# The first pass of a four-layer graph kernel multiplies h, turned, by the adjacency matrix, and its weights follow

## What is computed

```python
A2 = A + eye; dscale = diagonal(A2) ** -0.5
temp = A2 @ h @ W0.T                                   # pass 0
x = x + relu((dscale[:,None] * A2 * dscale[None,:]) @ temp)      # pass 1
g = h @ weight; gn = g / norm(g)
x = x + softmax(gn @ gn.T + log(adj + eps)) @ g + bias          # attention pass (2)
rowsum = adj.sum(axis=1); di = rowsum ** -0.5
x = x + relu((di[:,None] * adj * di[None,:]) @ h @ W + b)        # pass 3
# passes 4 and 5: two layers of relu(concat([h, adj @ h]) @ W), added to x once
```

## Time and profile before

| | us |
|---|---|
| runs, median of 3 (lowest to highest) | 2330.94 (2330.2 to 2331.07) |
| the profiled execution, its own time | 2330.06 |
| its span, first to last instruction | 2328.3 |
| pass 0, first product to the first of pass 1 | 21.89 to 390.28 |
| pass 1, to its last matmul | 390.28 to 741.31 |
| mean granted TensorE clock | 0.998 |

### The profile page before, as it was taken

One profiled execution on the slowest core, in us unless ns is written; L12 is line 12 of the kernel. 1 busy time (PEld: TensorE's weight loads), 2 busy tenths in 40 slices (PEclk: granted clock), 3 DMA queues, 4 the chain that ended last, 5 costly groups with the idle time before them and its releaser, 6 DMA issues.

```text
span 2328.3 us, 62880 instructions
## 1 busy us (share of the span) xinstructions
PE 2301.6 (99%) x24536; PEld 1937.0 (83%) x24536; DVE 1718.5 (74%) x2765; ACT 1130.9 (49%) x1821; POOL 140.3 (6%) x114
## 2 busy tenths in 40 slices
PE   7999999999999999999999999999999999999999
PEld 7888888666665677678888899999988888899998
DVE  7887876777776877678888876776776767666665
ACT  6644433454554555555555555555544444433332
POOL 2211101111010000000000000000000000000000
PEclk9999999999999999999999999999999999999999
DMA  8799998888987889989999998898898898999997
GB/s 288 218 359 340 356 357 305 253 270 272 275 266 222 252 294 286 277 282 305 330 312 327 330 363 307 327 342 304 327 345 320 333 339 301 340 347 378 375 371 292
DMA packets 291738, 726.86 MB, mean 312 GB/s; under 512 B 76704, under 2 KB 109728, under 8 KB 258848
## 3 DMA queue, kind: packets, MB, share of 16 engines
q1 hardware_dynamic: 291328, 724.42, 89.8%
q10 hardware_dynamic: 288, 0.79, 0.1%
HBM read 574.64 MB, written 138.41 MB: 306 GB/s over the span
## 4 chain that ended last, share of the span: by engine, by line
PE 91%; DVE 4%; issue 3%; POOL 1%; ACT 0%; POOLq 0%; DVEq 0%; ACTq 0%
PE acc L949 9%; PE acc L977 8%; PE acc L974 8%; PE acc L978 8%; PE acc L952 8%; PE acc L954 8%; PE acc L953 8%; PE acc L950 5%; PE acc L964 4%; PE acc L967 4%; PE acc L966 4%; PE psS L1198 2%; PE psS L1200 2%; PE psS L1199 2%; DVE alo L2115 1%
## 5 line engine op out<-in xcount | busy, mean ns | idle before, releaser
L952 PE MATMUL acc<-right,ahi 128*128 128x258 f16 x1536 | 420.0, 273 | 5.7 <-DVE alo L2115 2.3
L954 PE MATMUL acc<-right,alo 128*128 128x258 f16 x1536 | 419.9, 273 | 0.0
L953 PE MATMUL acc<-right,ahi 128*128 128x256 f16 x1536 | 419.3, 273 | 0.0
L974 PE MATMUL acc<-left,ahi 128*128 128x128 f16 x1536 | 270.4, 219 | 0.4 <-DVE alo L1746 0.4
L978 PE MATMUL acc<-left,alo 128*128 128x128 f16 x1536 | 270.4, 219 | 0.0
L977 PE MATMUL acc<-left,ahi 128*128 128x128 f16 x1536 | 270.4, 219 | 0.0
L1608 ACT ACTIVATE ahi<-en 128x512 f16<-128x512 f32 x256 | 160.2, 626 | 75.2 <-DVE en L2100 73.1
L952 PEld LDWEIGHTS acc<-right,ahi 128*128 128x128 f16 x1536 | 150.4, 98 | 38.2 <-DVE alo L2115 7.8
L949 PE MATMUL acc<-left,ahi 128*128 128x512 f16 x512 | 180.2, 379 | 0.0
L949 PE MATMUL acc<-left,en 128*128 128x512 f16 x512 | 180.2, 379 | 0.0
L978 PE MATMUL acc<-left,adj 128*128 128x128 f16 x1024 | 178.1, 219 | 0.0
(11 more groups left out here) (273 smaller groups left out, 6542.9 us busy)
## 6 DMA issues: line engine op xcount, KB each, us to landing
adj<-in_adj_t SPq DMA_DIRECT2D x192, 512.0 KB, 5.9
adj<-ready SPq DMA_DIRECT2D x96, 1024.0 KB, 7.7
en<-ready SPq DMA_DIRECT2D x96, 1024.0 KB, 8.1
adj<-in_adj_t SPq DMA_DIRECT2D x32, 1024.0 KB, 8.6
en<-in_adj_t SPq DMA_DIRECT2D x32, 1024.0 KB, 9.1
en<-ready SPq DMA_DIRECT2D x64, 512.0 KB, 5.2
en<-sent SPq DMA_DIRECT2D x46, 512.0 KB, 7.1
sent<-en SPq DMA_DIRECT2D x90, 256.0 KB, 4.3
```

The costliest lines, as they stand in the source:

```text
L952: nc.tensor.matmul(acc[:, b, 0:n], hi, m[:, jb, 0:n], start=first, stop=False)
L953: nc.tensor.matmul(acc[:, b, 0:F], hi, m[:, jb, LO:LO + F], start=False, stop=False)
L954: return nc.tensor.matmul(acc[:, b, 0:n], lo, m[:, jb, 0:n], start=False, stop=last)
L974: nc.tensor.matmul(to, hi[:, rows], bhi[:, cols], start=first and i % 2 == 0 and b == 0 and k == 0, stop=False, skip_group_check=True)
```

## The change

- Pass 0 multiplies by h itself. The block of h (128 rows x 128 features) is the stationary operand and adj's transpose the moving one, 512 columns at a time, so the result comes out turned, z = (adj h) transposed, in two banks per row group, and the row groups take the four banks in turn (`turned_block`). eye is added on PE by `own_rows`: 16 matmuls of 128 columns per row group by 256 times the identity. No transposes, no copy.
- z is split (ACT `hi_of_z`, DVE `lo_of_z`) at chunk 0 of the next row group, multiplied by W0 behind chunk 2 (24 matmuls), and the result, scaled by d, split at chunk 3 (`hi_of_t`, `lo_of_t`).
- The first two row groups (PAIRED) are taken in turn: each 512 rows of h serve a chunk of both. The statistics run one round ahead, and the splits of a round stand in front of the rows of the next. ACT makes the normalised rows of rounds 1 to 7 too.
- Pass 1 has the three matmuls of 258, 256 and 258 columns; the row sums move there, and with them POOL's power and `inverse_rows`; ACT alone takes its result out of the banks. CROSS and `add_cross` go.
- Two blocks of similarity (AHEAD) are made before the last chunk of pass 1.
- SP issues the first chunk at once, in two halves, and weights and diagonal between later chunks. keep_warm is 40 matmuls.

```diff
-WARM = [60, 60]
+WARM = 40
+PAIRED = 2
 LEAD = 3
+AHEAD = 2
...
+def pairs():
+    load_at(0)
+    load_x(1)
+    load_at(1)
+    load_at(2)
+    load_x(2)
+    load_at(3)
+    load_x(3)
+    for n in range(4, PAIRED * NC):
+        load_at(n)
+        if n < 8:
+            load_x(n)
+            load_weight(n - 4)
+        elif n == 8:
+            load_weight(4)
+            load_biases()
+        if n % 2 == 1 and n >= 9:
+            load_diagonal((n - 9) // 2)
+        store_whole(*place_of(n - 4))
...
-        both = m[:, jb, :].rearrange("p (s n) -> p s n", s=2)[:, :, 0:F]
-        nc.tensor.matmul(acc[:, b, :].rearrange("p (s n) -> p s n", s=2), hi, both, start=first, stop=False)
-        return nc.tensor.matmul(acc[:, b, 0:F], lo, m[:, jb, 0:F], start=False, stop=last)
     n = F + 2
     nc.tensor.matmul(acc[:, b, 0:n], hi, m[:, jb, 0:n], start=first, stop=False)
...
+def turned_block(g, n, c, k, f):
+    hi, lo = moving_of(n, k)
+    rows = mov[0][:, GB * c + k, :]
+    bhi, blo = rows[:, f * P:(f + 1) * P], rows[:, LO + f * P:LO + (f + 1) * P]
+    to = acc[:, 2 * (g % 2) + f, :]
+    nc.tensor.matmul(to, bhi, hi, start=c == 0 and k == 0, stop=False, skip_group_check=True)
+    nc.tensor.matmul(to, bhi, lo, start=False, stop=False, skip_group_check=True)
+    return nc.tensor.matmul(to, blo, hi, start=False, stop=False, skip_group_check=True)
+def own_rows(g):
+    for f in range(FB):
+        for b in range(GB):
+            rows = mov[0][:, GB * g + b, :]
+            to = acc[:, 2 * (g % 2) + f, b * P:(b + 1) * P]
+            nc.tensor.matmul(to, rows[:, f * P:(f + 1) * P], scaled_ident[:, :], start=False, stop=False,
+                             skip_group_check=True)
+            nc.tensor.matmul(to, rows[:, LO + f * P:LO + (f + 1) * P], scaled_ident[:, :], start=False, stop=False,
+                             skip_group_check=True)
+def first_pass():
+    for n in range(NG * NC):
+        g, c = place_of(n)
+        if n == 0:
+            pe.wait_ge(first_split, 1)
+        else:
+            pe.wait_ge(split_ready, n + 1)
+        if g == 0:
+            pe.wait_ge(mov_ready, at(MOVE, PRE, c, GB, 1 if c < 3 else GB))
+        if c == NC - 1:
+            if n == chunk_no(0, 0, NC - 1):
+                pe.wait_ge(scaled_ident_ready, 1)
+            own_rows(g)
+        for k in range(GB):
+            if g == 0 and c < 3 and k > 0:
+                pe.wait_ge(mov_ready, at(MOVE, PRE, c, GB, k + 1))
+            if n == 0 and k == GB // 2:
+                pe.wait_ge(split_ready, 1)
+            for f in range(FB):
+                if c == 0 and k == 0 and g >= PAIRED:
+                    pe.wait_ge(ev_ready, at(ALL, 0, g - 2, GB, 2 * f + 2))
+                last = turned_block(g, n, c, k, f)
+                if c == NC - 1 and k == GB - 1:
+                    last.then_inc(acc_ready, 2)
+        if c < NC - 1:
+            last.then_inc(chunk_done, 1)
+        if g >= PAIRED and c == 2:
+            if n == PAIRED * NC + 2:
+                pe.wait_ge(w_ready, 1)
+            step("W0W1", 0, g - 1 if g > PAIRED else 0)
+        if g == PAIRED and c == 6:
+            step("W0W1", 0, 1)
...
-            if tp in SMALL and tp != PRE and (c, b) in PLACES:
+            if p == 1 and isinstance(g, int) and g == NG - 1 and (c, b) == (NC - 2, GB - 1):
+                for j in range(AHEAD):
+                    similarity(0, j)
...
-keep_warm(WARM[0])
-pe.wait_ge(w_ready, 1)
-pe.wait_ge(ones_ready, 1)
-for s in ["T0T1", "W0", "W1"]:
-    step(s, PRE, 0)
-keep_warm(WARM[1])
-step("T0T1", PRE, 1)
+keep_warm(WARM)
...
+def hi_of_z(g, side):
+    if not (isinstance(g, int) and g == 0):
+        act.wait_ge(small_ready, at(SMALL, 0, g - 1, 2, 2))
+    for f in range(FB):
+        act.wait_ge(acc_ready, at(ALL, 0, g, GB, 2 * f + 2))
+        nc.scalar.activation(hTq[:, f, :, :], acc[:, 2 * side + f, :].rearrange("p (b n) -> p b n", n=P),
+                             ACT.Copy, scale=1.0 / ADJ_SCALE).then_inc(h_hi, GB // FB)
+def hi_of_t(g):
+    act.wait_ge(d_w_ready, 1)
+    for r in range(2):
+        act.wait_ge(small_ready, at(SMALL, 0, g, 2, r + 1))
+        for b in (2 * r, 2 * r + 1):
+            nc.scalar.activation(mov[1][:, blocks(g, b), 0:F], small_out(0, b), ACT.Copy,
+                                 scale=d_w[:, blocks(g, b)]).then_inc(mov_hi, 1)
...
+def first_rows(g):
+    act.wait_ge(shift_ready, at(NORM, PRE, g))
+    if g >= 2:
+        act.wait_ge(mov_ready, at(MOVE, PRE, g - 2, GB, GB))
+    u = g % 2
     for b in range(GB):
-        nc.scalar.activation(mov[1][:, blocks(g, b), 0:F], o[:, b, :], ACT.Copy, scale=d[:, blocks(g, b)])\
+        args = dict(bias=shift[:, u, b:b + 1], scale=rstd[:, u, b:b + 1])
+        nc.scalar.activation(mov[0][:, blocks(g, b), 0:F], xres[:, GB * g + b, :], ACT.Relu, **args)\
             .then_inc(mov_hi, 1)
+        if g > 0:
+            nc.scalar.activation(normed_of(g)[:, b, :], xres[:, GB * g + b, :], ACT.Identity, **args)\
+                .then_inc(normed, 1)
...
+TWO_PLACES = {0: ("z", 0), 3: ("t", 0), 4: ("z", 1), 7: ("t", 1)}
+def first_group(g, side):
+    for c in range(NC):
+        split(0, g, c)
+        if isinstance(g, int) and g == PAIRED:
+            if c in TWO_PLACES:
+                first_tail(*TWO_PLACES[c], TWO_PLACES[c][1])
+        elif c in FIRST_PLACES:
+            first_tail(FIRST_PLACES[c], g - 1, 1 - side)
+        if isinstance(g, int) and g == PAIRED + 1 and c == 5:
+            hi_of_weights(slice(wofs[1], wofs[5]), w_loaded, 16 * 5)
...
-stage("h", PRE, 0)
-hi_of_weights(slice(0, wofs[1]), w0_loaded, 16)
+act.wait_ge(const_ready, 1)
+nc.scalar.activation(rowm[:, :], neghalf[:, 0:GB], ACT.Copy)
 split(0, 0, 0)
+first_rows(0)
 for q in range(NG):
-    keep_hT(q, 0)
-    keep_hT(q, 1)
-    stage("W0", PRE, q)
-    if q == 0:
-        stage("W1", PRE, q)
+    split(0, 1, q)
     if q + 1 < NG:
-        stage("h", PRE, q + 1)
-    if q > 0:
-        stage("W1", PRE, q)
-    if q != 1:
-        split(0, 0, max(1, q))
-hi_of_weights(slice(wofs[1], wofs[5]), w_loaded, 16 * 4)
+        split(0, 0, q + 1)
+        first_rows(q + 1)
+    if q == NG - 2:
+        hi_of_weights(slice(0, wofs[1]), w_loaded, 16 * 5)
+first_group(PAIRED, 0)
+first_group(PAIRED + 1, 1)
+with act.Fori(PAIRED + 2, NG, 2) as g:
+    first_group(g, 0)
+    first_group(g + 1, 1)
...
+def lo_of_z(g, side):
+    for f in range(FB):
+        dve.wait_ge(h_hi, at(SMALL, 0, g, GB, 2 * f + 2))
+        nc.vector.scalar_tensor_tensor(hTq[:, FB + f, :, :],
+                                       acc[:, 2 * side + f, :].rearrange("p (b n) -> p b n", n=P), 1.0 / ADJ_SCALE,
+                                       hTq[:, f, :, :], ALU.mult, ALU.subtract).then_inc(ev_ready, GB // FB)
+    dve.wait_ge(ev_ready, at(ALL, 0, g, GB, GB))
...
+def lo_of_first_rows(g):
+    if g < 3:
+        for b in range(GB):
+            dve.wait_ge(normed, at(NORM, PRE, g, GB, b + 1))
+            dve.wait_ge(mov_hi, at(MOVE, PRE, g, GB, b + 1))
+            row = mov[0][:, GB * g + b, :]
+            nc.vector.scalar_tensor_tensor(row[:, LO:LO + F], normed_of(g)[:, b, :], 0.0, row[:, 0:F],
...
-for name in ["stats", "norm", "h"]:
-    stage(name, PRE, 0)
-lo_of_weights(slice(0, wofs[1]), 1)
+dve.wait_ge(const_ready, 3)
+nc.vector.tensor_scalar(scaled_ident[:, :], ident[:, :], ADJ_SCALE, None, ALU.mult).then_inc(scaled_ident_ready, 1)
+stage("stats", PRE, 0)
+split_first(0, first_split, first_hi)
+stage("norm", PRE, 0)
+lo_of_first_rows(0)
+split_first(1, split_ready, split_hi)
 stage("stats", PRE, 1)
-split(0, 0, 0)
 for q in range(NG):
-    if q == 0:
-        stage("W0", PRE, q)
-        stage("W1", PRE, q)
-    if q + 1 < NG:
-        stage("norm", PRE, q + 1)
     if q > 0:
-        stage("W0", PRE, q)
-    if q + 1 < NG:
-        stage("h", PRE, q + 1)
-    if q > 0:
-        stage("W1", PRE, q)
-    if q + 2 < NG:
+        split(0, 0, q)
+    if q == 1:
+        lo_of_first_rows(1)
+        stage("stats", PRE, 2)
+    elif q == 2:
+        stage("stats", PRE, 3)
+        lo_of_first_rows(2)
+    elif q > 2 and q + 2 < NG:
         stage("stats", PRE, q + 2)
-    if q != 1:
-        split(0, 0, max(1, q))
-lo_of_weights(slice(wofs[1], wofs[5]), 2)
+    split(0, 1, q)
+    if q == 2:
+        stage("stats", PRE, 4)
+    if q > 1 and q + 1 < NG:
+        lo_of_first_rows(q + 1)
+    if q == NG - 2:
+        lo_of_weights(slice(0, wofs[1]), 1)
 dve.wait_ge(diag_loaded, 16 * GB)
 nc.vector.tensor_scalar(diag[:, :], diag[:, :], 1.0, None, ALU.add).then_inc(diag_one, 1)
+dve.wait_ge(d_ready, 1)
+nc.vector.tensor_scalar(d_w[:, :], d[:, :], 1.0 / W_SCALE, None, ALU.mult).then_inc(d_w_ready, 1)
+first_group(PAIRED, 0)
+first_group(PAIRED + 1, 1)
+with dve.Fori(PAIRED + 2, NG, 2) as g:
+    first_group(g, 0)
```

(43 more changed lines are left out.)

346 lines of the change are left out of this document (174 added, 172 removed).

## The result

The changed kernel takes **2322.23 us** (median of 6 runs, 2321.43 to 2322.64) against 2330.32 (6 runs of before beside them): ratio 0.9965, 95% interval 0.9955 to 0.9975, 8.1 us faster. The forecast was 2323, with a range from 2314 to 2335. The profiled execution took 2322.25 us with a span of 2320.4.

A forecast was written before the change was run, and what follows sets the result against it. PE, busy in 99% of the span, was the bound. Terms 12.0 + 357.3 + 8.7 + 1.0 + 0.7 + 357.6 ended pass 1 at 737.3 against 741.4; with 3.5 at the next step, 7.6 us faster: 2323, range 2314 to 2335.

The forecast's parts named there:

- first product of pass 0: Start of the kernel: PE's first useful product at 12.0 us, bounds 10.7 and 13.5, 9.9 us sooner than before.
- stalls of the paired rounds: First two row groups of pass 0: PE waits 8.7 us together, bounds 3 and 17.
- half clock behind them: Pass 0's paired rounds: waits of 2 us and more may lower PE's clock, taken as 1.0 us.
- later row groups: Six later groups of pass 0: splits at chunks 1 and 4 cost 0.7 us, bounds 0 and 6.
- saved at the step to attention, clock included: From pass 1 to attention: 2.1 us of shorter wait and 1.4 of avoided half clock, 3.5 together.
- power of the diagonal: Ahead of row group 2: DVE waits for POOL's power of the diagonal, 5.43 us, costing PE 0.9.
- From the third round on DMA may set the pace: Paired rounds: splits wait for queued stores; stalls to round 4 are 5.3 us in all at 390 GB/s.
- the diagonal's four loads: nothing: Paired rounds 4 to 7: each load stands 4.4 us ahead of a store; costs nothing, or 4 if landing takes 12.
- What is left after the last chunk: ... 2.1 saved: Step to attention: 2.5 us remain after pass 1's last chunk, against 4.65 without the moved blocks.
- supply at 352 GB/s: Rival, paired rounds: loads and stores never go faster, stalls reach 17 us, 2333, about no change; chance 0.18.
- rounds set by handoffs: Rival, paired rounds: ACT and DVE waiting on each other make a round 12.8 us instead of 10.4; 2341; chance 0.10.
- No gain at the step: Rival, step to attention: PE waits as long for the exponential ahead of the last chunk as after it; 2326.5; chance 0.04.

The follow-up runs named there:

- e4: Changed kernel with x's first 512 KB issued by SP ahead of the first chunk, instead of by ACT beside it; 2321.31 us.
- e6: Changed kernel with ACT making a round's rows ahead of the split of its first chunk, from round 3 on, DMAs untouched; 2318.27 us.
- e7: Changed kernel with three edits: rows ahead of the split, diagonal's loads at chunks 12 to 15 and biases at 12, x's first rows ahead on SP; 2315.76 us.
- e10: e7 with DVE's lo of the second chunk put ahead of round 1's statistics, its sums behind them; 2317.75 us.
- e3: Changed kernel with the diagonal's four loads at chunks 12 to 15 (before 9, 11, 13, 15) and biases at 12 (before 8); 2319.59 us.
- e1: Changed kernel with AHEAD = 0, no block of similarity before the last chunk of pass 1; 2322.72 us.
- e8: Kernel before, with pass 1 by three matmuls of 256 columns and DVE's addition gone, similarity blocks left behind pass 1; 2329.91 us.
- e5: Kernel before, with only AHEAD = 2 added: two similarity blocks before the last chunk of pass 1; 2327.93 us.
- e2: Changed kernel with the five weight loads (1.75 MB) issued with chunks 9 to 13 of the pairs instead of 4 to 8; 2321.99 us.
- e9: Changed kernel with two edits: rows ahead of the split from round 3 on, and x's first rows ahead of the first chunk on SP; 2317.57 us.

## Why the prediction was right, point by point

The sum of the profiled executions, forecast and measured:

| term | forecast | measured |
|---|---|---|
| first product of pass 0 | 12.0 | 12.97 |
| PE's work in pass 0 | 357.3 | 357.2 |
| stalls of the paired rounds | 8.7 | 6.66 |
| half clock behind them | 1.0 | 1.40 |
| later row groups | 0.7 | 0.68 |
| PE's work in pass 1 | 357.6 | 358.0 |
| end of pass 1, without the moved blocks | 737.3 | 736.9 |
| saved at the step to attention, clock included | 3.5 | 3.4 |

The measured work of pass 0 is 378.90 - 12.97 less the 8.74 of the three rows below it; that of pass 1 is 739.30 - 378.90 less 2.38 for the moved blocks. The step is 2.38 + 2.46 = 4.84 us for 6.95, 2.1 saved, and 1.3 of clock. Against the kernel before, the first product comes 8.9 us sooner, PE's work of pass 0 is 3.2 shorter (360.4 by the prediction's sum) and its waits 0.7 longer, pass 1 is 6.9 longer, and the step with its clock 3.4 shorter: 7.9 in all, the difference of the two spans.

Part of the match is luck: the start came 1.0 us later than forecast and the stalls of the paired rounds 2.0 shorter, and the half clock behind them, forecast with 1.0, was 1.40 in this execution and 0 in others with longer stalls (e4).

- **PE's work** held to 0.1 us in pass 0: 512 columns with h stationary take 0.216, and `own_rows` 0.89 us a group for the forecast 0.90. Over passes 0 and 1 together PE's work grew, as argued; the gain is at the start and at the step to attention.
- **The start** was 1.0 us later, and one term has it: sharing the engines with the first chunk was taken as 1.2 us and cost 2.2 (x's statistics at 6.56 for 4.39). POOL's power took 2.04 for the forecast 2.3. The 40 matmuls of no use took 4.05 us, from 8.92 to 12.97, and ended about 0.2 behind the first rows' lo (about 12.8, as DVE's lo of the rows starts at 12.23 and PE followed that start by 0.56 to 0.57 wherever it waited for it: e4, e6, e7, e10).
- **The stalls by hand**: second chunk 1.17 for 1.6, rows of round 2 0.87 for 0.9, later rounds 4.62 (0.17, 1.53, 2.92) for 5.3, power of the diagonal 0 for 0.9, since PE came to row group 2 that late (105.74). Once PE was through with the pairs 5.5 us sooner (100.26 in e6), this wait was there with 2.2.
- **Later groups**: the 0.15 to 0.21 us stand at chunk 4, whose split waits behind `hi_of_t`, and none at chunk 1. The term had both places; one of them was nothing.
- **A sign of failure that came.** The prediction was to fail if the rounds of the pairs were over 12 us apart. They start at 12.97, 24.51, 35.93, 47.81 and 61.10: the first three distances are under 12, and so are those behind 61.10, but the fourth is 13.3. In one round the working did not hold, and that is the round of the first point below.

Two steps came near in size and were wrong in cause.

- "From the third round on DMA may set the pace" was priced as bytes over a rate. The rate of 390 GB/s was near for the bytes ahead of that split (399 from 13 to 48 us, 355 from 48 to 62), and e6 shows that supply does set the moment of chunk 8's split. But with the DMAs untouched e6 lost both stalls: 4.1 us of rows on ACT and 1.2 of their lo on DVE stood between that moment and PE. I had these in the hand count and still named the supply as the cause; they were an order that could be changed. The step "the diagonal's four loads: nothing" failed too: with the biases they cost 1.3 us of stall and, in this execution, the 1.4 of half clock (e3). SP's queue and the rate point to the diagonal, but it was not moved without the biases.
- "What is left after the last chunk: ... 2.1 saved" put the gain of the step to attention down to the moved blocks. The 2.5 us left behind the last chunk were right (2.46); wrong was the 4.65 without the moved blocks, which took all of the old step for the chain through the exponential. In e1, without them, it is 5.07 - 2.38 = 2.69. e1 shows 0.26 us of them with the addition gone, e8 1.9 us and the clock for the missing addition with no moved block, e5 1.1 and the clock for the blocks alone. The addition's own wait stood in the earlier trace rows with its 2.1 us, and in my working it was only "waits".

Of the rivals, supply at 352 GB/s was too slow for 13 to 48 us (399), where most of the bytes ahead of the stalls moved; only from 48 to 62 us did the core come down to it (355). The rule beside it, about 358 GB/s, did not bind there: another page of the Trainium skill (HBM Reference, Specifications (TRN2)) says that a core streaming alone measures about 425 GB/s. That agrees with this kernel on one core, whose loads ran at 407 to 425. The slower case, rounds set by handoffs, had its mechanism right (DVE waits for rows with a split behind it) and its price wrong: only one round of eight grew by over 1.9 us. "No gain at the step" was wrong, as the step gained 3.4 us, but right in that the blocks gave nearly nothing of it.

## What to carry to other kernels

When an engine waits for a transfer with other ready work behind it, do the ready work in the wait: e6 moved no byte and gained 4.0 us. A part of a stall can be put down to a cause only by an edit that leaves the other causes alone; moving the bytes (e2) or the start (e4) only moved the stalls. And where two edits shorten the same wait, price each with the other in place.

## What the runs showed of the hardware

- **A short stall may or may not cost clock.** Behind stalls of 2.92 us (changed kernel) and 2.51 (e1) the granted clock was at half for about 3 us: in the one from the first matmul behind the stall, in the other from 1.1 to 1.4 us later. Behind 3.02 and 3.37 us (e4) and 2.20 (e6) it stayed at full. The length of the one stall doesn't decide it, and what does was not found. From 61 to 64 us in e4, with the stall of 3.37 us in front of 61.66:

```profile
61.00:64.00 3.00, 2.34 (x11) 1.09 (x12) 2.81 (x12) 1.89 (x2) 0.19 (x1) 1.00 1.11 350
```

- **The first products can run at half clock, at no cost here.** In e1, e2, e3, e4 and e9 the first one to four products start up to 0.43 us apart, twice the 0.216; in the changed kernel, e6, e7 and e10 none does. The window's PEclk reads 1.00 there all the same, so the distances tell more. It cost nothing that stayed, as PE waits for the second chunk behind it: that stall is 0.45 us in e1 for 1.17 in the changed kernel, and the second chunk starts at 19.37 for 19.32.
- **A scattered load can hold the queue for what stands behind it, and the rate is lower beside it.** The diagonal's first load was issued in 0.48 us and the 256 KB store behind it in 7.07, against 0.43 without it. Behind the three others that issue took 2.95, 2.00 and 1.85 us, and 1.09 to 3.19 in e3. From 41 to 49 us the core moved 367 GB/s, and 422 in e3, where neither the diagonal nor the biases stand there. A store with no small transfer right in front could stand 2.82 as well (e3, 35.67), so not all of such a time is the scattered load's.
- **Two queues share the engines from the first byte.** With 512 KB of x beside the 1 MB of the first chunk, x's statistics began 2.2 us later than with x nearly alone (6.56 for 4.39). Ahead of the chunk in one queue x was there at 4.50 to 4.81 (e4, e7, e9, e10), and the first half chunk reached ACT at 7.00 to 7.95, for 7.71 in the changed kernel.
